# Attention: the value product of each step moved between the two pairs of score products

## What is computed

```python
x_ln = layer_norm(x_flat, g1, beta1)
q, k, v = jnp.split(x_ln @ w_qkv.T, 3, axis=-1)
q, k, v = (to_heads(q), to_heads(k), to_heads(v))
scores = jnp.einsum('bhqd,bhkd->bhqk', q, k) * HEAD_DIM ** (-0.5)
attn = jax.nn.softmax(scores, axis=-1)
out = jnp.einsum('bhqk,bhkd->bhqd', attn, v)
```

## Time and profile before

| what | value |
|---|---|
| median of 3 executions | 3674.92 us (3674.7 to 3675.24) |
| profiled execution, from first to last instruction | 3666.4 us |
| the median less that span | 8.5 us |
| PE busy | 3163.0 us (86%) |
| DVE busy | 2573.4 us (70%) |
| POOL busy | 2214.4 us (60%) |
| ACT busy | 2006.1 us (55%) |
| attention, from the first to the last score product (timeline) | 102 to 1973 us |

### The profile page before, as it was taken

The page is one execution under the profiler, slowest core; times in us unless marked ns, Lnnn a source line. Parts: engine busy times, 40 slices in busy tenths (PEclk is TensorE's granted clock), DMA queues, the critical chain, the costliest instruction groups (busy, mean ns, idle before and its releaser), DMA issues. The chain is left out here.

```text
span 3666.4 us, 55668 instructions
## 1 busy us (share of the span) xinstructions
PE 3163.0 (86%) x18550; PEld 1183.9 (32%) x18550; DVE 2573.4 (70%) x3346; ACT 2006.1 (55%) x2381; POOL 2214.4 (60%) x684
## 2 busy tenths in 40 slices
PE   6999999999999999999995899774888888887787
PEld 2333333333333333333331233341322222222222
DVE  5777777777767777777771222142888988988988
ACT  3566666666656666666663333223555564565554
POOL 0577777777777777777776000003657666666666
PEclk7899999999999999999998999886989999999999
DMA  2000000000000000000003211114333433443443
GB/s 103 12 16 10 16 16 16 16 13 16 16 17 10 16 16 16 19 10 16 16 10 74 92 69 46 48 64 149 119 132 128 155 142 120 153 150 118 147 150 115
DMA packets 74739, 234.86 MB, mean 64 GB/s; under 512 B 13088, under 2 KB 14180, under 8 KB 74420
## 3 DMA queue, kind: packets, MB, share of 16 engines
q1 hardware_dynamic: 69460, 215.06, 17.3%
q0 software_dynamic: 5056, 16.83, 1.3%
HBM read 192.42 MB, written 39.39 MB: 63 GB/s over the span
## 5 line engine op out<-in xcount | busy, mean ns | idle before, releaser
L526 DVE TENSOR_REDUCE at_pmax<-at_ring 128x1 f32<-128x512 f32 x2048 | 1300.8, 685 | 392.0 <-PE at_ring L334 381.2
L479 ACT ACTIVATE at_probs<-at_sc 128x1024 f32<-128x1024 f32 x1024 | 992.5, 1021 | 531.7 <-PE at_sc L402 529.7
L580 POOL TENSOR_TENSOR at_prob_sums<-at_prob_sums,at_probs 128x2048 f32<-128x2048 f32 x256 | 1159.0, 4527 | 74.8 <-ACT at_probs L479 54.5
L398 PE MATMUL at_sc<-at_QT,at_KT 32*128 32x512 f32 x4096 | 782.5, 634 | 4.1 <-issue 3.7
L1634 POOL TENSOR_TENSOR ss_drive<-ss_du,ss_bsb 128x1024 f32<-128x1024 f32 x261 | 610.7, 2352 | 263.9 <-DVE ss_state L1591 257.1
L1534 ACT ACTIVATE ss_decay<-ss_delta,ss_a 128x512 f32<-128x512 f32 x520 | 354.5, 687 | 447.6 <-DVE ss_state L1587 299.5
L410 PE MATMUL at_O<-at_probs,at_V 128*32 128x512 f32 x4096 | 535.3, 606 | 52.5 <-DVE at_att L549 51.6
L580 POOL TENSOR_TENSOR at_prob_sums<-at_probs 128x2048 f32<-128x2048 f32 x64 | 290.7, 4543 | 403.1 <-ACT at_probs L479 403.1
L1423 PE MATMUL ss_Y<-ss_seen,ss_ident 128*128 128x512 f32 x1032 | 520.7, 628 | 0.0
L334 PE MATMUL at_ring<-at_KH,at_QH 32*128 32x512 bf16 x2048 | 442.3, 387 | 5.7 <-DVE at_pmax L526 2.9
L1599 DVE TENSOR_TENSOR ss_seen<-ss_state,ss_C 128x1024 f32<-128x1024 f32 x259 | 316.3, 1221 | 80.4 <-PE ss_C L1411 72.6
(11 more groups left out here) (199 smaller groups left out, 2695.6 us busy)
## 6 DMA issues: line engine op xcount, KB each, us to landing
ss_bsb<-scratch_rows SPq DMA_DIRECT2D x265, 512.0 KB, 6.9
scratch_attn<-at_att SPq DMA_DIRECT2D x64, 256.0 KB, 2.0
fc_att<-scratch_attn SPq DMA_DIRECT2D x32, 512.0 KB, 5.8
ss_xn<-scratch_xm SPq DMA_DIRECT2D x34, 256.0 KB, 5.6
at_xn<-scratch_xn SPq DMA_DIRECT2D x32, 256.0 KB, 3.8
ss_xw<-scratch_xw SPq DMA_DIRECT2D x17, 256.0 KB, 3.9
ln_x<-in_x SPq DMA_DIRECT2D x8, 512.0 KB, 4.2
scratch_xn<-ln_xn POOLq DMA_DIRECT2D x8, 512.0 KB, 3.0
```

The source lines that it names most:

```text
L398: nc.tensor.matmul(sc[:, h, :], KT[head(h), par, blk(kb)], QT[head(h), par, hs(half)], start=True, stop=False)
L479: nc.scalar.activation(probs[:, kb, two, :].rearrange("p h q -> p (h q)"), sc[:, two, :].rearrange("p h q -> p (h q)"), ACT.Exp, scale=SCA ...
L526: nc.vector.tensor_reduce(pmax[:, quad // 2, h, quad % 2:quad % 2 + 1], ring[:, unit[3], :], AX_X, ALU.max, negate=True).then_inc(max_done, 1)
L580: nc.gpsimd.tensor_tensor(prob_sums[:, half, :, :], before, probs[:, k, :, :], ALU.add).then_inc(pool_sums, 1)
```

## The change

`scores` is called twice in a step, for heads 0 and 1 and for heads 2 and 3. The call of `values` moves from behind the first two maxima (and the extra unit) to between the two calls. Ahead of it stands a wait for both exponentials of the step before. Steps without a value product get no such wait. Nothing else changes.

```diff
-            def scores(stage, grp, par, s):
+            def scores(stage, grp, par, s, heads):
                 half, kb = divmod(s, KB)
-                if kb == 0:
+                if kb == 0 and heads[0] == 0:
...
-                for h in range(GH):
+                for h in heads:
...
                     if stage != "lead":
-                        scores(stage, grp, par, s)
+                        scores(stage, grp, par, s, (0, 1))
+                        if not (stage == "first" and s == 0) and s % KB != 1:
+                            pe.wait_ge(exp_done, 2 * (STEPS * grp + s))
+                        if s == 0:
+                            if stage != "first":
+                                values(grp - 1, 1 - par, STEPS - 1)
+                        elif s % KB == 2:
+                            values(grp, par, s - 2)
+                            values(grp, par, s - 1)
+                        elif s % KB != 1:
+                            values(grp, par, s - 1)
+                        scores(stage, grp, par, s, (2, 3))
                     maxima(stage, grp, par, s, (0, 1))
...
-                    if stage != "lead":
-                        if s == 0:
-                            if stage != "first":
-                                values(grp - 1, 1 - par, STEPS - 1)
-                        elif s % KB == 2:
-                            values(grp, par, s - 2)
-                            values(grp, par, s - 1)
-                        elif s % KB != 1:
-                            values(grp, par, s - 1)
                     maxima(stage, grp, par, s, (2, 3))
```

## The result

The changed kernel takes **5523.48 us** (median of 3, 5494.96 to 5533.82) against 3674.92: 1.5016 times as long, with a 95% interval of 1.4958 to 1.5073. The forecast was 4418, with a range up to 4620. The direction was right, the size was not: of 1849 us more, the forecast had 743.

The account below looks back on a forecast made before the run. The attention was taken as bound by a chain through PE's single stream, feeding ACT and DVE too late. Periods of 81.8 us against 58.18 lose 731 us over 31, plus 12 for the last: about 4418 us, range 4200 to 4620.

Parts of the forecast that it names:

- lost cover: With four maxima together, the fourth waits for its ring bank and holds back the next scores: 1.20 us.
- special steps: Steps of a period with other waits, 12.3 us together, which may be off by a third, 127 us either way.
- step 1: Step of a period without a value product, order kept; it starts earlier against DVE's casts and waits: 6.54 us.
- step 10: Step whose double value product waits for the sums to be taken out, row maxima and second pair behind it: 6.40 us.
- plain step: Eight steps of each period: 3.23 us to the second pair's row terms plus 1.20 of ring wait, 4.43 us.
- The ring rival: The fourth maximum's bank is free in time; second pair, ACT and value product decide: 3.44 us steps, about 4030 us, chance 0.09.
- The hole is filled: The value product fills PE's 142 waits for ACT, if a lone pair costs about 0.5: 3550 us, chance 0.04.
- two restarts: Two places where PE restarts at half clock; thinner work may take longer to win it back: up to some 30 us.
- The clock falls: PE idles about a fifth of a step; half clock in half of the steps: 740 us more, 5160, chance 0.07.
- theory C: From the experiments: the array's work over time sets the clock, and products of few rows give little; no chance given.
- A: From the experiments: PE's idle time behind the fourth maximum's wait lowers the clock; no chance given.
- B: From the experiments: lone score pairs, using half of the array's rows, lower the clock, to near 0.64; no chance given.

Follow-up runs that it names:

- e_fill_wait: The changed kernel with three unused full-array products ahead of the fourth maximum's wait for its bank: 4520.92 us, 1.2311 times the kernel before.
- e_ring_only: The kernel before with the value product straight behind the four scores and all four maxima behind it: 4062.19 us, 1.1067 times.
- e_ring_free: The changed kernel with the first two maxima ahead of the value product for heads 2 and 3, the last two for heads 0 and 1: 4190.61 us.
- e_part_max: The kernel before with score pairs parted by the first two maxima, for heads 2 and 3, and the value product in its old place: 3957.53 us.
- e_fill_thin: The changed kernel with three unused products of 32 rows behind the fourth maximum's wait for its bank: 5909.63 us, 1.61 times the kernel before.
- b_lead1: The kernel before with one unused full-array product ahead of each maximum of the lead-in: 3697.36 us, 1.0068 times.
- e_fill_wait_thin: The changed kernel with three unused products of 32 of 128 rows ahead of the fourth maximum's wait for its bank: 5084.52 us, 1.3845 times the kernel before.

## Why the prediction was right in part, and where it failed

**What bounds, and the prices: right.** PE's single stream sets the step, a pair is as dear as four heads, and the lost cover turns into a wait for DVE. At full clock the changed step is 4.52 (4.43), and the wait after the row terms 1.29 (1.20). With the clock held up by one added product, a period is 82.3, against 81.8 forecast. Some luck is in that: errors of special steps cancel. In `e_fill_wait`, its added products included, step 1 takes 7.18 (1569.19 to 1576.37; 6.54 forecast) and step 10 5.96 (1618.09 to 1624.05; 6.40 forecast), with the double V 1.86 after P0 and not 2.38. An estimate of the changed order at full clock, from `e_fill_wait` less 31 times the 2.73 of two added products, is 4436 us (one product's cost is still in it), close to the forecast of 4418. Of the 763 us that this is above the kernel before (3673), the ring's wait with whole scores accounts for 390; the rest, some 370, is what the parting adds, 0.87 in a plain step.

**The ring rival** asked for steps of 3.44. It is what the last period does, which has few maxima left; V then waits for ACT:

```profile
3761.58 1.15 PE L398 MATMUL at_sc<-at_QT,at_KT 32*128 32x512 f32 x8
...
3764.05 1.06 PE L410 MATMUL at_O<-at_probs,at_V 128*32 128x512 f32 x8 [1.10 <-ACT at_probs L481]
3765.04 1.15 PE L398 MATMUL at_sc<-at_QT,at_KT 32*128 32x512 f32 x8
```

3.46 from step to step. The rival was sound, but it governs one period in 32. **The rival "The hole is filled"** asked for a lone pair of about 0.5; it took 0.96.

**The step that failed is the full clock.** The forecast priced every product at full clock, and put the loss of it at up to 30 us, at two restarts, where "thinner work may take longer to win it back". That slow return came in almost every half of a period. The rival "The clock falls" had 0.07 and a price of 740 us, by half of the steps. It came, and it cost about 1003, by the estimate above some 1090: a plain step at half clock takes 3.19 more (7.71 against 4.52; 2.9 had been said), and half clock held for some 72% of the attention, not half. Forecast and rival together, 5160, would have come nearer; the 360 missing are nearly all clock.

Two arguments had put it aside. The first was the earlier trace rows: in a later layer PE was busy only 2.35 of 5 us and kept 1.00. The row doesn't say which products those were. They are of 128 rows, and two of 96:

```profile
2986.51 0.60 PE L1411 MATMUL ss_C<-ss_bc,ss_select 96*128 96x512 bf16 x2 [1.48 <-DVE ss_seen L1599]
2986.95 1.88 PE L1423 MATMUL ss_Y<-ss_seen,ss_ident 128*128 128x512 f32 x4
```

It was read as a proof about busy time, and so it said nothing of products of 32 rows. In the changed kernel the clock fell in a stretch with PE busy 2.32 of 2.50.

The second was the Trainium skill, "TensorE: Matmul & The Clock Gate", Part 1: the clock falls after the engine was idle. The trace disagrees in this case: no wait ahead of a fall is longer than about 1.2 us, and at 0.50 PE goes on for tens of microseconds without winning the clock back, busy for most of every 2.5 us. Of products of few rows that part says nothing; "not after thin work" was the prediction's own reading. The same part of the Trainium skill, in its section "A second HAM failure mode: psum-queue depth-cycling", tells of a kernel that cycles through PSUM banks and whose clock swings between the levels for many short idles; the prediction passed it over. The swing is here. Short idles alone don't account for it: `e_ring_only` cycles through the same banks, idles 18% and keeps 0.99, with eight falls in its attention.

What the runs show in its place agrees with theory C, and not with A or B alone. The step's products are the same in four kernels. Spread over 3.48 to 3.65 us (`e_ring_free`, `e_ring_only`, `e_part_max`) they keep a clock of 0.94 to 0.99; spread over 4.52, in the changed kernel, 0.64. Full-array products added to the 4.52 bring it back, whether they fill the idle time (1.00) or not (0.95); thin ones don't (0.78 and 0.64). So the two costs come together: the parted pairs and the ring's wait make the step longer with no more work in it, and it is the kernel with both that loses the clock. Why the chip lowers it there stays open.

## What to carry to other kernels

A unit that stands between users of a small ring of banks is their cover; moved away, it shows as a wait that holds back the next step's scores as well (390 us here). Products on different row groups shared the array here while nothing that needs all rows came between them: four heads took 0.96 together, and each pair 0.96 with V in between. And before a change that makes a stream of thin products looser, give the clock a rival with a real chance: a PE that reads as busy can still lose half its speed, and a cheap test is to put a full-array product that nobody needs into the new hole.

## What the runs showed of the hardware that I had not expected

- PE's busy share doesn't tell the clock: it was 0.99 with PE idle 18% (`e_ring_only`), and 0.64 with PE idle 7% and thin added products (`e_fill_thin`).
- The clock doesn't come back merely because PE is busy: in `b_lead1` PE was busy 19.53 of each 20 us between 80 and 120 with full products among thin ones, and the clock stayed at 0.50; in the changed kernel 58 of the 97 rises came with the denominators.
- Products of rows that a pair of scores leaves free run beside it, also where they stand behind it in the program: the thin products of `e_fill_wait_thin` started 0.42 after P1 (1515.43 to 1515.85), with P1's row terms still to come.
- Useless work can pay: one product per step in the hole took the changed kernel from 5523 to 4554 us.
